# Cross-attention with a router layer, one core: the way into the pair loop rebuilt (input sums beside the value tiles, six key weight buffers, two product cycles interleaved)

## What is computed

```python
xn = layernorm(x)
q, k, v = xn @ Wq, ctx @ Wk, ctx @ Wv      # heads 32, 8, 8
q, k = rope(q, pos), rope(k, pos)          # q*cos + rotate_half(q)*sin
p = softmax(where(mask == 0, -1e9, q @ k.T / sqrt(128)))
x = x + (p @ v) @ Wo
h = layernorm(x)
s = softmax(h @ router.T + bias); top 8 of 64 kept as w_dense
x = x + h * w_sum + w_dense @ expert_bias
```

## Time and profile before

| | |
|---|---|
| time, median of 3 (lowest, highest) | 630.6 us (630.49, 632.16) |
| the profiled execution's own time | 630.11 us |
| its span in the trace | 628.3 us |
| PE busy | 589.3 us (94%) |
| VectorE, ScalarE, GpSimd busy | 485.2 (77%), 397.9 (63%), 417.2 us (66%) |
| DMA mean | 72 GB/s |

### The profile page before, as it was taken

How to read it: one execution, slowest core, us unless ns; L and a number is a source line. 1 busy time by engine, 2 the same in 40 slices (tenths; PEclk the granted TensorE clock), 3 DMA queues, 4 the chain that set the end, 5 groups by cost and what they waited for, 6 DMA issues and landing times.

```text
span 628.3 us, 10559 instructions
## 1 busy us (share of the span) xinstructions
PE 589.3 (94%) x2980; PEld 491.2 (78%) x2980; DVE 485.2 (77%) x796; ACT 397.9 (63%) x1054; POOL 417.2 (66%) x386
## 2 busy tenths in 40 slices
...
PEclk9999989799899999999999999999999999999997
...
GB/s 287 348 219 153 60 116 145 40 35 1 117 33 36 51 85 51 52 36 64 67 33 100 46 20 50 83 50 50 50 50 67 15 86 18 18 17 1 35 33 69
DMA packets 30817, 45.40 MB, mean 72 GB/s; under 512 B 3008, under 2 KB 11328, under 8 KB 30784
## 3 DMA queue, kind: packets, MB, share of 16 engines
...
## 4 chain that ended last, share of the span: by engine, by line
PE 68%; DVE 10%; issue 7%; POOL 6%; ACT 4%; DMA 2%; SPq 2%; DVEq 0%; ACTq 0%; POOLq 0%
PE outp L1584 8%; PE outp L1586 8%; PE outp L1585 8%; PE score L1565 8%; PE bank_a L1438 4%; PE bank_a L1440 4%; PE bank_a L1439 4%; PE probT L1597 4%; POOL rot L486 2%; DMA v_dram<-v_stage 2%; PE attnT L1426 2%; PE attnT L1424 2%; PE attnT L1425 2%; PE bank_c L1440 2%; PE bank_c L1438 2%
## 5 line engine op out<-in xcount | busy, mean ns | idle before, releaser
L486 POOL TENSOR_TENSOR rot<-rot,sinT 128x512 f32<-128x512 f32 x80 | 109.6, 1370 | 63.9 <-ACT rot L725 63.8
L875 ACT ACTIVATE probs<-score,negmax 128x128 f32<-128x128 f32 x256 | 91.1, 369 | 31.6 <-DVE negmax L1208 31.6
L601 POOL TENSOR_TENSOR probs<-probs,rsum 128x512 f32<-128x512 f32 x64 | 69.1, 1080 | 51.2 <-DVE rsum L1214 51.2
L1584 PE MATMUL outp<-wo_hi,oT_hi 128*128 128x512 f32 x240 | 95.5, 398 | 2.1 <-DVE oT_lo L1233 1.3
L1586 PE MATMUL outp<-wo_hi,oT_lo 128*128 128x512 f32 x240 | 93.8, 391 | 0.0
L1585 PE MATMUL outp<-wo_lo,oT_hi 128*128 128x512 f32 x240 | 93.5, 389 | 0.0
L1221 DVE TENSOR_TENSOR resid<-resid,outp 128x512 f32<-128x512 f32 x60 | 41.0, 684 | 53.1 <-PE outp L1586 53.1
L1065 DVE TENSOR_TENSOR qT<-qT,rot 128x512 f32<-128x512 f32 x57 | 69.8, 1224 | 6.1 <-POOL rot L486 3.5
L1565 PEld LDWEIGHTS score<-kT,qT 128*128 128x128 f32 x512 | 66.7, 191 | 5.8 <-issue 1.0
L1565 PE MATMUL score<-kT,qT 128*128 128x128 f32 x512 | 67.5, 275 | 0.6 <-ACT probs L875 0.6
L1438 PE MATMUL bank_a<-x_hi,w_hi 128*128 128x512 f32 x128 | 55.5, 434 | 9.7 <-ACT part_s L748 2.7
...
## 6 DMA issues: line engine op xcount, KB each, us to landing
...
```

The source lines that it names most:

```text
L486: pool.tensor_tensor(rot[:, k0 % 2, :], rot[:, k0 % 2, :], sinT[:, half * W:(half + 1) * W], ALU.mult).then_inc(sin_done, 1)
L601: pool.tensor_tensor(probs[:, p], probs[:, p], rsum[:, p, :].unsqueeze(2).broadcast_to([P, GH, S]), ALU.mult).then_inc(soft_done, 1)
L875: last = act.activation(probs[:, p, h, :], heads(score[p][:, :])[:, h, :], ACT.Exp, bias=negmax[:, p, h:h + 1], accum_out=sums[:, p, h:h + 1])
L1584: pe.matmul(ps[:, :], oT_hi[:, cols], w[0], start=h == 0, stop=False)
```

## The change

`WK` goes from 4 to 6 buffers, as a list placed at 112, 116, 120, 124, 106 and 102 KiB. Cycles 0 and 1 get banks and `part_*` buffers of their own (`banks_of`, `parts_of`), and their products alternate. x tiles are normalised, transposed and copied in pairs after value tiles 8 to 11. All of `hi_x` and 11 of the 14 `lo_x` stand ahead of the key tiles. The four first `lo_wo` go from VectorE to GpSimd. On SyncE the loads of v move behind `store_k(11)`, those of pair 2 from `k == 7` to `k == 4`, and key weights 6 and 7 are loaded among the value stores. The ropes of cycles 0 and 1 are all done ahead of step 0. The diff, cut to its core ("..." marks what is left out; the rest of the edits only pass the new buffers on, or drop a wait of cycle 1 on cycle 0 that the second set of buffers makes needless):

```diff
-WK = 4
+WK = 6
...
-wk_hi = at("wk_hi", [WK, C, D], F32R, 112)
-wk_lo = at("wk_lo", [WK, C, D], F32R, 120)
+wk_at = 112, 116, 120, 124, 106, 102
+wk_hi = [at(f"wk{r}_hi", [C, D], F32R, o) for r, o in enumerate(wk_at)]
+wk_lo = [at(f"wk{r}_lo", [C, D], F32R, o + 2) for r, o in enumerate(wk_at)]
...
+parts = [(part_s, part_t, part_u),
+         (at("part_s1", [W], F32, 160), at("part_t1", [W], F32, 162), at("part_u1", [W], F32, 168))]
...
+cycle_banks = [(bank_a, bank_b, bank_c), (outp0, probT, attnT)]
...
-        if i in (9, 10, 11, 12):
+        if 9 <= i < 9 + KV - RA:
             load_wk(RA + i - 9)
...
-    for i in range(VS):
-        sp.wait_ge(dma_vout[i], 16 * len(range(i, KB * B, VS)))
-    for half in range(NH):
-        load_v(0, half)
     sp.wait_ge(x_ps, B)
     for h in range(2):
         load_wo(0, h)
-    load_wk(6)
-    store_k(2)
-    load_wk(7)
-    for k in range(3, KK):
+    for k in range(NH, KK):
         store_k(k)
+        if k == 4:
+            load_pair(2, 0)
         if k == 7:
-            load_pair(2, 0)
             sp.wait_ge(a_lo, PIECES * PAIR)
             for h in range(2, GH):
                 load_wo(0, h)
-    for i in range(KS):
-        sp.wait_ge(dma_kout[i], 16 * len(range(i, KK - NH, KS)))
+        if k == 11:
+            for i in range(VS):
+                sp.wait_ge(dma_vout[i], 16 * len(range(i, KB * B, VS)))
+            for half in range(NH):
+                load_v(0, half)
     load_pair(3, 0)
     load_pair(4, 0)
...
-        if k == 11:
+        if k == 9:
             sums12(2, 0)
-        if k == 13:
+        if k == 10:
             sum3(2, 0)
+            sum4(2, 0)
         if k == 14:
-            sum4(2, 0)
+            lo_v(0, 0)
...
+    lo_wo(0, 0)
+    lo_wo(0, 1)
+    lo_w(W0, 2, 0)
     rotate((KK, 0, 0), 0)
-    lo_w(W0, 2, 0)
     rotate((KK + 1, 0, 0), 0)
+    lo_wo(0, 2)
+    lo_wo(0, 3)
+    rotate((KK + 2, 0, 0), 1)
+    rotate((KK + 3, 0, 0), 0)
     lo_w(W3, 2, 0)
-    rotate((KK + 2, 0, 0), 0)
+    rotate((KK + 4, 0, 0), 0)
     lo_w(W1, 2, 0)
-    rotate((KK + 3, 0, 0), 0)
+    rotate((KK + 5, 0, 0), 1)
     lo_w(W2, 2, 0)
-    lo_v(0, 0)
-    rotate((KK + 4, 0, 0), 1)
+    rotate((KK + 6, 0, 0), 1)
+    sums12(3, 0)
     soften(0, 1)
-    rotate((KK + 5, 0, 0), 1)
-    sums12(3, 0)
+    lo_w(W0, 3, 0)
     soften(1, 2)
-    rotate((KK + 6, 0, 0), 1)
-    lo_w(W0, 3, 0)
-    sum3(3, 0)
-    sum4(3, 0)
-    lo_w(W3, 3, 0)
-    lo_w(W1, 3, 0)
...
-        if b == 0 and not last:
+        if first and b == 0:
+            sum3(3, 0)
+            sum4(3, 0)
+        elif b == 0 and not last:
             lo_w(W2, 3, g)
...
+        if first and b == 0:
+            lo_w(W3, 3, 0)
+            lo_w(W1, 3, 0)
+        if first and b == 1:
+            lo_w(W2, 3, 0)
...
+    hi_w(W0, 1, 0)
+    hi_w(W3, 1, 0)
     act.wait_ge(proj_done, U_V + B)
-    for j in range(B):
+    for j in range(0, B, 2):
+        if j == 0:
+            hi_wk(0)
         copy_x(j)
-        if j < WK:
-            hi_wk(j)
+        copy_x(j + 1)
         if j == 0:
-            hi_w(W0, 1, 0)
-            hi_w(W3, 1, 0)
-        if j == 1:
             hi_w(W1, 1, 0)
             hi_w(W2, 1, 0)
-        if j == 4:
+            hi_wk(1)
+        if j == 2:
+            hi_wk(2)
             hi_x(B11, 0)
             hi_x(B21, 0)
             hi_x(B22, 0)
-        if j == 6:
-            hi_x(T1, 0)
-            hi_x(T2, 0)
-            hi_x(T3, 0)
-            hi_x(T4, 0)
+        if j == 4:
+            hi_wk(3)
+    hi_x(T1, 0)
+    hi_x(T2, 0)
+    hi_x(T3, 0)
+    hi_x(T4, 0)
+    hi_wk(4)
+    hi_x(B11, 1)
+    hi_x(B21, 1)
+    hi_x(B22, 1)
+    act.wait_ge(a_lo, PIECES)
+    hi_wk(5)
+    hi_x(T1, 1)
+    hi_x(T2, 1)
+    hi_x(T3, 1)
+    hi_x(T4, 1)
+    def hi_v(g, half):
+        act.wait_ge(dma_v[half], 16 + g * 16)
+        act.activation(v_hi[:, half, :], v_raw[:, half, :], ACT.Copy).then_inc(vhi_done, 1)
...
     act.wait_ge(dma_vout[VS - 1], 16 * len(range(VS - 1, KB * B, VS)))
-    keep_s(0, 0)
     hi_wo(0, 0)
     hi_wo(0, 1)
+    keep_s(0, 0)
+    hi_w(W0, 2, 0)
+    keep_s(1, 0)
     swap_c11(0, KK, 0)
+    swap_c11(1, KK + 1, 0)
     keep_t(0, 0)
-    hi_w(W0, 2, 0)
-    keep_u(0, 0)
-    act.wait_ge(a_lo, PIECES)
-    hi_v(0, 0)
-    swap_c21(0, KK + 1, 0)
-    keep_s(1, 0)
-    hi_w(W3, 2, 0)
+    keep_t(1, 0)
     hi_wo(0, 2)
     hi_wo(0, 3)
-    swap_c11(1, KK + 2, 0)
-    keep_t(1, 0)
+    keep_u(0, 0)
+    swap_c22(0, KK + 2, 0)
+    keep_u(1, 0)
+    swap_c21(0, KK + 3, 0)
+    hi_w(W3, 2, 0)
+    swap_c21(1, KK + 4, 0)
     hi_w(W1, 2, 0)
-    keep_u(1, 0)
     hi_w(W2, 2, 0)
-    swap_c21(1, KK + 3, 0)
+    swap_c12(0, KK + 5, 0)
     keep_s(2, 0)
-    swap_c22(0, KK + 4, 0)
+    swap_c22(1, KK + 6, 0)
     keep_t(2, 0)
     exps(0, 1, True)
     keep_u(2, 0)
+    hi_w(W0, 3, 0)
     exps(1, 2, True)
-    swap_c12(0, KK + 5, 0)
-    hi_w(W0, 3, 0)
-    hi_w(W3, 3, 0)
-    swap_c22(1, KK + 6, 0)
-    hi_w(W1, 3, 0)
-    hi_w(W2, 3, 0)
...
+        if first and b == 0:
+            hi_w(W3, 3, 0)
+            hi_w(W1, 3, 0)
+            hi_w(W2, 3, 0)
...
-        if i == X_AFTER - 2:
+        if i == X_AFTER - 1:
             dve.wait_ge(rstd_done, 1)
             dve.wait_ge(b_lo, KB * C)
-        if 0 <= i - X_AFTER + 2 < B:
-            normalise_x(i - X_AFTER + 2)
+        if X_AFTER - 1 <= i < X_AFTER - 1 + HB:
+            normalise_x(2 * (i - X_AFTER + 1))
+            normalise_x(2 * (i - X_AFTER + 1) + 1)
         if X_AFTER < i <= X_AFTER + WK:
             lo_wk(i - X_AFTER - 1)
-        if i >= KB * B - 2:
+        if i == KB * B - 3:
             for j in range(3):
-                lo_x(3 * (i - KB * B + 2) + j, 0)
+                lo_x(j, 0)
+        if i == KB * B - 2:
+            for j in range(3, 7):
+                lo_x(j, 0)
+        if i == KB * B - 1:
+            for j in range(4):
+                lo_x(j, 1)
...
         if half == NH - 1 and g + WK < KV:
             lo_wk(g + WK)
-        if k == 0:
-            lo_x(6, 0)
-        if 5 <= k < 12:
-            lo_x(k - 5, 1)
+        if k < 3:
+            lo_x(k + 4, 1)
...
-    for i in range(KS):
-        dve.wait_ge(dma_kout[i], 16 * len(range(i, KK - NH, KS)))
+    def stored(slot):
+        dve.wait_ge(dma_kout[slot], 16 * len(range(slot, KK - NH, KS)))
+    stored(0)
     make_c11(0, 0)
+    stored(3)
+    make_c11(1, 0)
     rope_query(hold[:, 0, :], 0, KK, 0, 0, 0)
+    rope_query(hold[:, 3, :], 1, KK + 1, 0, 0, 0)
     rope_query(None, 0, KK, 0, 0, 1)
+    rope_query(None, 1, KK + 1, 0, 0, 1)
+    stored(1)
     make_c22(0, 0)
-    rope_query(bank_a[:, :], 2, KK + 1, 0, 0, 0)
+    rope_query(hold[:, 1, :], 2, KK + 2, 0, 1, 0)
+    make_c22(1, 0, KK + 2)
+    rope_query(None, 2, KK + 2, 0, 1, 1)
+    rope_query(bank_a[:, :], 2, KK + 3, 0, 0, 0)
+    rope_query(outp0[:, :], 3, KK + 4, 0, 0, 0)
+    stored(2)
     make_c12(0, 0)
-    rope_query(None, 2, KK + 1, 0, 0, 1)
-    make_c11(1, 0)
-    for h in range(2):
-        first_wo(h)
-    rope_query(hold[:, 3, :], 1, KK + 2, 0, 0, 0)
-    rope_query(None, 1, KK + 2, 0, 0, 1)
-    make_c22(1, 0, KK + 3)
-    rope_query(bank_a[:, :], 3, KK + 3, 0, 0, 0)
     make_c12(1, 0)
-    rope_query(None, 3, KK + 3, 0, 0, 1)
-    for h in range(2, GH):
-        first_wo(h)
-    make_c11(2, 0, KK + 1)
+    rope_query(None, 2, KK + 3, 0, 0, 1)
+    rope_query(None, 3, KK + 4, 0, 0, 1)
+    rope_query(hold[:, 2, :], 0, KK + 5, 0, 1, 0)
     mask_scores(0, 0, 1)
     row_max(0, 1, True)
-    rope_query(hold[:, 1, :], 2, KK + 4, 0, 1, 0)
+    make_c11(2, 0, KK + 1)
+    rope_query(None, 0, KK + 5, 0, 1, 1)
+    invert_sums(0, 1, True)
     mask_scores(1, 1, 2)
     row_max(1, 2, True)
-    rope_query(None, 2, KK + 4, 0, 1, 1)
-    invert_sums(0, 1, True)
+    rope_query(hold[:, 3, :], 3, KK + 6, 0, 1, 0)
+    rope_query(None, 3, KK + 6, 0, 1, 1)
     invert_sums(1, 2, True)
...
-        if first and b == 0:
-            rope_query(hold[:, 2, :], 0, KK + 5, 0, 1, 0)
-            rope_query(None, 0, KK + 5, 0, 1, 1)
-            rope_query(hold[:, 3, :], 3, KK + 6, 0, 1, 0)
-            rope_query(None, 3, KK + 6, 0, 1, 1)
...
-        if 0 <= i - X_AFTER < B:
-            transpose_x(i - X_AFTER)
+        if X_AFTER <= i < X_AFTER + HB:
+            transpose_x(2 * (i - X_AFTER))
+            transpose_x(2 * (i - X_AFTER) + 1)
...
     m1(0, 0, U_K + KK - 3)
     pe.wait_ge(proj_free, U_K + KK - 2)
     m2(0, 0)
+    m1(1, 0, U_K + KK - 1)
+    pe.wait_ge(x_copied, B)
+    m2(1, 0)
     m6(0, 0)
+    m6(1, 0)
     pe.wait_ge(proj_free, U_K + KK)
     m5(0, 0)
     m7(0, 0)
-    m2(1, 0)
+    m5(1, 0)
+    m7(1, 0)
     m4(0, 0)
+    m4(1, 0)
     m3(0, 0)
-    m1(1, 0, U_K + KK + 2)
-    m5(1, 0)
-    m6(1, 0)
-    m2(2, 0)
-    m7(1, 0)
-    m4(1, 0)
     m3(1, 0)
     m1(2, 0, U_K + KK + 4)
+    m2(2, 0)
+    pe.wait_ge(rope_done, KK + GH + 1)
+    scores(0, 0, True)
     m6(2, 0)
-    scores(0, 0, True)
     m7(2, 0)
```

(29 more changed lines are left out.)

39 lines of the change are left out of this document (17 added, 22 removed).

## The result

The changed kernel takes 612.19 us (median of 5 runs, 611.18 to 615.61), the kernel before 630.60 us (5 runs, 630.46 to 632.16). The ratio is 0.9716, with a 95% interval of 0.9699 to 0.9733: 18.4 us faster, where 23.7 us were forecast (607.0). The profiled execution happens to be the slowest of the five: 615.61 us, a span of 613.7 us. Its ledger is therefore some 3 us worse than the median.

The account below looks back on a forecast made before the run. PE was taken to set the pace from about 168 us, with the loop unedited. Terms +2.1 - 6.3 - 11.2 - 8.3 = -23.7 us took 630.1 to 606.4, plus 0.5 for the median: 607, range 600 to 617.

Parts of the forecast that it names:

- What bounds it: Whole kernel: PE sets the pace from about 168 us, so the gain is how far the first output matmul moves.
- Cycle 2 and step 0: -8.3: From cycle 2's next product to the first output matmul: 28.3 us become 20.0, with 2.0 for handoffs not followed.
- The value stage: +2.1: Before the keys: later normalised tiles and a wait behind hi_wk(2) start the first key near 58.2, 2.1 us later.
- VectorE's backlog in front of the keys: 0: Before the first keys: VectorE's queued lo_x and lo_wk end at 66.5, hidden before key 4, costing 0 us.
- The key stage: -6.3: The 16 key tiles: 49.79 us become 43.5, as waits on ropes and the slow matmuls behind them go.
- no PE wait on ropes between keys: Key stage, a sign to look for: PE never waits for a rope between keys; such waits were 3.8 us before.
- Backlog: Rival, chance 0.12: dear lo_x and lo_wk keep the key stage at its 49.8 us, giving 613 us.
- Cycles 0 and 1: -11.2: From the first product to cycle 2's next: 34.2 us become 23.0, since interleaved products cover each other's waits.
- Moves that cost nothing: Reordered loads, including v behind store_k(11), and the four lo_wo leaving VectorE: no cost counted.
- GpSimd tight: Cycles 0 and 1: GpSimd is the tightest engine, its 21st rope ending at 123.5, just when scores(0) is due.
- The sum: Start to first output matmul: the stage terms add to -23.7 us, moving that matmul from 168.4 to 144.7.

Follow-up runs that it names:

- e3: Changed kernel with the split of the first v tile moved from keys 13 and 14 to behind the last key's swap; 609.39 us.
- e8: Changed kernel with VectorE's lo_p of step 0 put ahead of make_c22, the mask and the maximum; 610.89 us.
- e6: Changed kernel with eight extra matmuls of unused result on PE where it would be idle ahead of value tile 9; 610.71 us.
- e5: Changed kernel with ScalarE's hi_wk(2) and hi_wk(3) put behind the copies of x that GpSimd's sums need; 608.31 us.
- e1: Changed kernel with the value and key stages put back as before the change, keeping the new cycles and step 0; 611.59 us.
- e7: Changed kernel with the edits of e3, e4 and e5 together; 605.79 us.
- e4: Changed kernel with x tiles 0 and 1 normalised ahead of the copy that waits for the store; 608.88 us.

## Why the prediction was right, and where it was off

**What bounds it** was right. PE is full from the marker on, the loop is untouched, and the marker alone tells the result: moved by 14.56 us, the span by 14.6 (628.3 - 613.7). The gain came where PE had waited longest, and the new wait for `pT_lo` is 2.4 us against 2.3 forecast.

**"Cycle 2 and step 0: -8.3"** measured -10.4. The 2.0 us added for handoffs not followed weren't needed: 17.9 us against 16.2 counted plus 1.8 for the clock.

**"The value stage: +2.1"** was mis-sized, +4.25 in the profiled execution. Two terms were too small. The normalised tiles beside GpSimd took 0.98 us each, not 0.6, and the store released VectorE 0.5 us later than before (its copy starts at 32.52, not 32.03), so PE was idle 1.98 + 0.21 = 2.2 us, not 0.7; and behind that idle time came the low clock, 4.05 us for a tile of 2.72, which I had only as a bound. One was too large: the feared wait behind `hi_wk(2)` was real on ScalarE (3.3 us) but cost PE only 0.45, not 1.9. These three make 1.4 of the 2.15 us of error, and the rest wasn't traced. In e3 and e8, which have the same value stage, the keys started at 58.16 and 58.92, near the forecast 58.2: this term differs from one execution to the next by about 2 us.

**"VectorE's backlog in front of the keys: 0"** is the step that failed in the profiled execution. I put the `x_lo` near the low price, since "GpSimd's sums end near 56 and its first rotation starts near 62". The sums ended at 60.9, for I had followed the late weights 2 and 3 only to PE's transposes and not on to `copy_x` 6 and 7, on which GpSimd's sums wait; that cost 2.2 us. And by my own times the `x_lo` lasted until 66.5, 4.5 us beyond the start of that rotation, and I had put no price on that; beside rotations and query weights they cost 3.8 us more. The `x_lo` took 1.17 us on average, the backlog reached its high bound, and PE waited 1.8 us at key 4 and 0.5 and 1.1 later. In e3, e6 and e8 the first `times_cos` came 10.0 to 10.3 us behind the first key, not 8.3 as forecast but still ahead of key 4 (4 x 2.72 = 10.9): there the 0 held, narrowly.

**"The key stage: -6.3"** became -2.1, mostly by these waits. Without the one at key 4 it is 46.14 us in e8, -3.7: the 0.9 and 1.1 us for ropes are there too, where I had expected "no PE wait on ropes between keys". e5 takes all but 0.3 us of them away, and its key stage needs 44.1 us. The rival "Backlog" thus happened in part. Its 613 lies nearer to the measured 612.2 than the forecast's 607 does, but the key stage did not keep its 49.8 us, and more than half of what was missed lies in other stages.

**"Cycles 0 and 1: -11.2"** was -6.4. Two causes. One is "Moves that cost nothing": "Should v be late, ScalarE's swap of key 14 stands behind it" was named and given no price. v came 2 us late, and its place in the order held the last ropes even where it wasn't (e1); e3 gained 2.8 us. The other is the chain of ropes, splits and copies through GpSimd, VectorE and ScalarE, which by hand came out with `part_t` "ready at 110.3 for a product due at 111.4" and in truth ended 2.1 us late. How much of this is the term "GpSimd tight" and how much ScalarE's order was not separated; e7, with no late v and early ropes, still needs 25.9 us for these cycles against 23.0, 1.9 of them the wait for `part_u`. In the profiled execution the low clock behind `part_t` adds 1.2 us (2.56 for a product of 1.36).

**The sum.** In the profiled execution the errors are +2.15, +4.2, +4.8 and -2.1, which make 9.1 us: -14.6 for -23.7. That the 2.0 us set aside for handoffs in step 0 made up for a part of what was missed elsewhere is luck. The median of the runs, 612.19, lies 3.4 us below that execution, so the forecast of 607 is 5.2 us off, and e3, e4 and e5 together take out 6.4: with them the kernel runs in 605.8.

**Still open.** Which of several short waits the 25.9 us of e7's cycles would lose with a lighter GpSimd. Putting `lo_wo` back on VectorE on top of e7 wasn't tried.
